# The place of the attention step in a unit of TensorE's queue: between the gate and the down products instead of behind the up products

## What is computed

```python
x = x + attn_ref(cond_ref(x, W1, b1, v, prompt), W_kv_down, W_k_up, W_v_up, W_q, W_q_rope, W_k_rope, W_o)
h = einsum('bsd,bdh->bsh', x, W[cats]) + b[cats][:, None, :]
...
def body(acc, ws):                       # over the 64 experts
    wg, wu, wdn, cw = ws
    hmid = silu(h @ wg) * (h @ wu)
    return (acc + cw[:, None] * (hmid @ wdn), None)
...
x = x + y + silu(h @ Ws_gate) * (h @ Ws_up) @ Ws_down
```

## Time and profile before

| what | us |
|---|---|
| runs | 753.29, 755.12, 757.13; median 755.12 |
| the profiled execution | 754.2 |
| its span, first to last instruction | 752.4 |
| PE busy in the span | 721.2 (96%) |
| DVE, ACT, POOL busy | 547.1, 453.3, 425.5 |
| mean granted clock of TensorE | 0.989 of full speed |

### The profile page before, as it was taken

The page is one execution under the profiler, slowest core; times in us unless marked ns, Lnnn a source line. Parts: engine busy times, 40 slices in busy tenths (PEclk is TensorE's granted clock), DMA queues, the critical chain, the costliest instruction groups (busy, mean ns, idle before and its releaser), DMA issues.

```text
span 752.4 us, 15834 instructions
## 1 busy us (share of the span) xinstructions
PE 721.2 (96%) x5644; PEld 556.2 (74%) x5644; DVE 547.1 (73%) x1150; ACT 453.3 (60%) x872; POOL 425.5 (57%) x349
## 2 busy tenths in 40 slices
PE   4788989999999999999999999999999999999997
PEld 3576767777787777777787777777777777877885
DVE  3867666886688856976778866888569766886664
ACT  2656875477555775567655775556755675555553
POOL 2456864555455655566455664566456555566665
PEclk8899999999999999999999999999999999999999
DMA  7494344434454364444545345443644344345451
GB/s 262 143 340 116 112 123 113 138 98 127 121 117 134 103 142 112 128 112 117 121 128 131 102 144 121 105 121 109 151 114 131 105 122 126 100 124 148 127 135 47
DMA packets 69055, 97.20 MB, mean 129 GB/s; under 512 B 8017, under 2 KB 26897, under 8 KB 68977
## 3 DMA queue, kind: packets, MB, share of 16 engines
q1 hardware_dynamic: 64512, 91.21, 44.8%
q10 hardware_dynamic: 4464, 4.98, 1.9%
HBM read 90.73 MB, written 4.98 MB: 127 GB/s over the span
## 4 chain that ended last, share of the span: by engine, by line
PE 75%; ACT 9%; DVE 8%; POOL 4%; issue 2%; DMA 1%; POOLq 0%; DVEq 0%; SPq 0%; ACTq 0%
PE Y L950 21%; PE U L950 20%; PE G L950 20%; PE A L950 12%; POOL hid_lo L613 2%; ACT s_t L378 2%; DVE act_w L921 2%; ACT hid_hi L517 2%; ACT L505 1%; DVE hid L933 1%; PE A L1011 1%; ACT L378 1%; ACT G L505 1%; DMA pooled_scratch<-hid 1%; DMA w<-in_weights 1%
## 5 line engine op out<-in xcount | busy, mean ns | idle before, releaser
L613 POOL TENSOR_TENSOR hid_lo<-hid,hid_hi 128x512 fp32r<-128x512 f32 (+1 forms) x264 | 342.2, 1296 | 277.5 <-ACT hid_hi L517 276.7
L921 DVE TENSOR_TENSOR act_w<-G,cwb 128x512 f32<-128x512 f32 x248 | 170.4, 687 | 99.8 <-ACT G L505 98.0
L505 ACT ACTIVATE G<-G 128x512 f32<-128x512 f32 x248 | 144.4, 582 | 149.3 <-PE G L950 147.5
L517 ACT CAST hid_hi<-hid 128x512 fp32r<-128x512 f32 (+1 forms) x264 | 162.3, 615 | 64.3 <-DVE hid L933 63.5
L933 DVE TENSOR_TENSOR hid<-act_w,U 128x512 f32<-128x512 f32 (+1 forms) x256 | 175.7, 686 | 23.4 <-PE Y L950 1.5
L950 PE MATMUL G<-c_hi,wg_hi 128*128 128x512 f32 x248 | 113.6, 458 | 0.0
L950 PE MATMUL Y<-hid_hi,wd_hi 128*128 128x512 f32 (+1 forms) x264 | 106.6, 404 | 5.3 <-POOL hid_lo L613 5.0
L950 PE MATMUL Y<-hid_hi,wd_lo 128*128 128x512 f32 (+1 forms) x264 | 103.5, 392 | 0.0
L950 PE MATMUL Y<-hid_lo,wd_hi 128*128 128x512 f32 (+1 forms) x264 | 103.5, 392 | 0.0
L950 PE MATMUL U<-c_hi,wu_hi 128*128 128x512 f32 x248 | 98.4, 397 | 0.0
L950 PE MATMUL G<-c_hi,wg_lo 128*128 128x512 f32 x248 | 97.7, 394 | 0.0
(11 more groups left out here) (183 smaller groups left out, 894.7 us busy)
## 6 DMA issues: line engine op xcount, KB each, us to landing
cwb<-cw_scratch SPq DMA_DIRECT2D x256, 256.0 KB, 3.7
k_blk<-in_cond_w SPq DMA_DIRECT2D x112, 64.0 KB, 2.3
wg_raw<-in_we_gate SPq DMA_DIRECT2D x8, 256.0 KB, 6.1
wu_raw<-in_we_up SPq DMA_DIRECT2D x8, 256.0 KB, 6.2
wd_raw<-in_we_down SPq DMA_DIRECT2D x8, 256.0 KB, 6.7
xf<-in_x_feat SPq DMA_DIRECT2D x8, 256.0 KB, 4.2
out_feat<-y ACTq DMA_DIRECT2D x8, 256.0 KB, 2.2
h_feat<-pooled_scratch SPq DMA_DIRECT2D x7, 256.0 KB, 2.7
```

The source lines that it names most:

```text
L505: nc.scalar.activation(gate_bank(p)[:, :], gate_bank(p)[:, :], ACT.Silu).then_inc(S["silu_done"], 1)
L517: nc.scalar.copy(hid_hi[0:n, p % NH, :], hid[0:n, p % NH, :]).then_inc(S["hi_ready"], 1)
L613: nc.gpsimd.tensor_sub(hid_lo[0:n, p % NH, :], hid[0:n, p % NH, :], hid_hi[0:n, p % NH, :].bitcast(F32)).then_inc(S["lo_ready"], 1)
L921: nc.vector.tensor_mul(act_w[:, p % NH, :], gate_bank(p)[:, :], cwb[:, p % NCW, :])\
```

## The change

In the PE part of a unit the two lines that issue the attention step move from the end of the unit to the place behind the gate product. Nothing else changes: the other engines keep their instructions and their order.

```diff
                 three(gate_bank(p)[:, :], wg_hi[:, p, :], wg_lo[:, p, :], c_hi[par][:, :], c_lo[par][:, :], True, True)\
                     .then_inc(S["gate_done"], 1)
+                for step, blk in steps_in(p, following, last):
+                    attention_step(step, blk)
                 if p >= NH:
                     down(b, p - NH)
                 elif prev:
                     down(b - 1, UNITS + p - NH)
...
                     three(up_bank(p)[:, :], wu_hi[:, p, :], wu_lo[:, p, :], c_hi[par][:, :], c_lo[par][:, :], True, True)\
                         .then_inc(S["up_done"], 1)
-                for step, blk in steps_in(p, following, last):
-                    attention_step(step, blk)
```

## The result

| | before | changed |
|---|---|---|
| median of 4 runs, us | 755.16 (753.29 to 757.13) | 793.37 (792.86 to 793.86) |
| ratio, 95% interval | | 1.0506 (1.0478 to 1.0533) |
| the profiled execution, us | 754.2 | 792.86 |
| its span, us | 752.4 | 791.0 |
| mean granted clock | 0.989 | 0.984 |

The account below looks back on a forecast made before the run. TensorE (PE), busy 721.2 of 752.4 us, was taken as the bound. Six later blocks at 5.46 us (32.8) plus 6.2 in the first gave 39.0 us on 754.2: 793 us, range 777 to 806.

Parts of the forecast that it names:

- step 17, att: Attention step in unit 12: PE waits 0.77 us for DVE's att, ready at E + 1.46; 0.11 added for the restart.
- step 19, x_next: Attention step: PE waits 0.89 us for DVE's result of the step before, ready at E + 1.58; 0.11 added.
- step 21, c: Attention step: PE waits 0.88 us for c, made by DVE one step earlier; 0.11 added for the restart.
- step 6, rope mask: Attention step in unit 1: PE waits 0.48 us for DVE's rope mask, ready at E + 1.17; 0.11 added.
- step 5, q_grp: Attention step in unit 0: PE waits 0.56 us for ACT's fourth q_grp, 0.67 with the restart.
- step 31, cw: PE waits 0.68 us for DVE's cw, kept late by routing; plus 0.11, less 0.10: 0.69.
- steps 13 and 14: Units 8 to 10: about 1.7 us wait for the first probability copy, partly given back at hid_lo; 0.64 us lost.
- E: Moment when a unit's up products have all been issued; PE was to reach the moved step at E + 0.69.
- the restart: PE's first product after a wait: 0.50 us long and not 0.39, so 0.11 added per wait, 0.44 for four.
- Only the DVE waits are real: Rival: the ACT and routing waits vanish, seven times 3.46 us stays: 778 us; chance 0.18.
- The clock falls: Rival: one clock fall of 1.5 us in each of seven blocks, 804 us, or 814 with a second; chance 0.12.
- Faster: Rival: earlier steps and later down products remove all hid_lo waits, 5.0 us: 749.2 us; chance 0.03.

Follow-up runs that it names:

- the fifth experiment: Changed kernel, with results PE waits for made ahead of hid on DVE and, for q_grp, ahead of the rounding on ACT: 771.42 us against 754.41, ratio 1.0219.
- eighth experiments: Kernel before the change, with only attention steps 16 to 21 moved behind the gate: 775.09 us against 756.27, ratio 1.0259.
- the third experiment: Kernel before the change, with only attention steps 5, 13, 14, 31 and 32, released by ACT or routing, moved behind the gate: 771.59 us, ratio 1.0197.
- the second experiment: Kernel before the change, with only attention steps 6, 17, 19 and 21, which wait for DVE, moved behind the gate: 765.81 us, ratio 1.0133.

## Why the prediction was right, point by point

The side, the mechanism and the time were right: 793 forecast, 793.37 measured. But the sum behind it was not right in every term. That the point was met to half a microsecond is luck: errors cancel. Per later block, in us:

| term | predicted | measured, by the gates |
|---|---|---|
| step 17, att | 0.88 | 0.78 |
| step 19, x_next | 1.00 | 0.79 |
| step 21, c | 0.99 | 0.86 |
| step 6, rope mask | 0.59 | 0.37 |
| step 5, q_grp | 0.67 | 0.68 |
| step 31, cw | 0.69 | 0.72 |
| steps 13 and 14 | 0.64 | 0.60 |
| the block | 5.46 | about 4.75 |

Small terms make up the rest of the last line: step 7 gives back 0.1 in unit 2, and steps 31 and 32 cost a little more in units 27 and 28.

**The waits themselves** came as written. Less the 0.16 us that the view hides, 0.77 (att), 0.89 (x_next), 0.88 (c), 0.48 (rope mask), 0.56 (q_grp) and 0.68 (cw) become 0.61, 0.73, 0.72, 0.32, 0.40 and 0.52; the brackets of the block shown above are 0.60, 0.70, 0.70, 0.30, 0.39 and 0.50. The fifth and eighth experiments tie them to DVE's and ACT's order and to the distance from E.

**The mis-sized terms of a later block** are the restart and the price of the waits at steps 6 and 19. For the restart the prediction says "so I add 0.11 to each". A 0.50 us product follows an attention step in either place: before, it was the gate behind the step, as in the earlier trace rows (360.27 and 364.11), now it is the down product. It was moved and not added. Of the four steps that wait for DVE only 17 and 21 take longer themselves behind their wait, by 0.06 and 0.10 from their start to the next group's: 0.16 us a block, and not 0.44. Steps 6 and 19 are rows of 32 small products. PE takes 0.32 us, and not 0.23, from the start of a 512-column product to the first of them in the kernel before too, where it waits for nothing:

```profile
377.27 0.39 PE L950 MATMUL U<-c_lo,wu_hi 128*128 128x512 f32 x1
...
377.59 1.08 PE L950 MATMUL A<-k_blk,x_next 128*32 128x128 f32 x32
```

So the wait there costs some 0.1 less than its length: 0.35 and not 0.48 at step 6, 0.77 and not 0.89 at step 19. The two together are most of the 0.7 by which a block was set too high.

**The first block** was set too high as well: 6.2 us, where 4.7 are measured without the fall of the clock (next paragraph). The 1.38 for "the products moved behind the wait" of step 13 left out that PE waited for hid_lo in front of the down products of units 7 and 8 in the kernel before, 0.25 us in the one and 0.69 in the other:

```profile
95.86 0.50 PE L950 MATMUL Y<-hid_hi,wd_hi 128*128 128x512 f32 x1 [0.69 <-POOL hid_lo L613]
```

These waits are gone in the changed kernel, so units 7 to 9 lose about 0.65 there and not 1.38.

**What made up for it.** The sum without these errors is 28.3 us in the later blocks and 4.7 in the first: 33 us, or 787. Two falls of the clock bring 4.0, and an opening that was 1.7 us longer in this execution the rest. The prediction had "so I take no fall", and a reading of 0.50 inside the blocks among its signs of a wrong sum; the sign came in two blocks. These are windows of the changed kernel at the fall in the first block (two), at that in a later one, and over steps 17 to 21 of this later block, where three waits follow one another without a fall:

```profile
100.00:101.00 1.00, 0.00 (x0) 0.00 (x0) 0.90 (x2) 1.00 (x3) 0.00 (x0) 0.56 0.00 0
...
104.00:107.00 3.00, 3.00 (x8) 2.29 (x8) 0.87 (x3) 0.00 (x0) 2.62 (x4) 0.51 0.70 154
...
380.00:382.50 2.50, 2.50 (x8) 1.92 (x7) 1.47 (x4) 1.10 (x2) 2.12 (x2) 0.50 0.63 176
...
393.00:406.00 13.00, 11.60 (x81) 8.67 (x79) 6.92 (x11) 5.79 (x11) 5.15 (x4) 1.00 0.39 102
```

The 0.5 in the first three is the level of 1.2 GHz; 0.56 is the mean of a stretch in which the clock falls. Both falls go with the wait of step 13. In the first block it begins while PE still waits, and PE then works at half speed: from the start of step 13 to that of step 14 PE takes 5.59 us (101.47 to 107.06), and 3.15 in a later block without a fall (286.80 to 289.95), so it costs 2.4 us. The later one costs 1.5: units 8 and 9 of its block are that much longer than in the others. The wait in the first block is

```profile
101.47 1.09 PE L1011 MATMUL A<-c,s_t 128*128 128x128 f32 x4 [4.08 <-ACT pt_sb L387]
```

It is longer than the 1.77 of the earlier trace rows by the down and up products that stood in front of it, which come behind it now, as the prediction says of the first block, and by the wait for hid_lo that stood in front of that down product.

**The rivals.** *Only the DVE waits are real* falls: the third experiment alone has 2.0 us a block from the others. *The clock falls* in every block falls as well: it fell in 2 of 7. *Faster* was wrong for the change as a whole, but the piece of it that the prediction names, the hid_lo waits, is there: they shrink from 5.0 to 1.3 us, and where steps 7 and 14 alone are moved and the copy comes first, the kernel gains 0.4 to 0.9%. *No effect* falls with the result.

**The expectation that missed by most**, 773 to 777 for the second experiment, failed by one step: the working took PE's arrival at E + 0.69 from the changed order, in which nothing but the gate lies between, and that held only if the step before is early as well.

## What to carry to other kernels

Before an instruction is moved forward in the queue of the engine that sets the pace, write down when its inputs are made and what that hangs on: if a result is made behind something that waits for the same engine's previous group, it needs a fixed time after that group, and the work in between is what hides it. Count the distance in issue times from that release and count every step that lies between. Where only some of the moved steps have inputs that are ready early, move those alone, and bring the late input forward on the engine that makes it.

## What the runs showed of the hardware

**The clock behind a wait isn't decided by the wait's length alone.** At the 4.1 us wait of the first block it fell in all three kernels that have it. Behind the wait of about 1.8 us that eight others have at the same place it fell in three and stayed at 1.00 in five, the kernel before among them; one of 2.5 us (step behind the down products) had no fall. At step 5 of the first block PE waits 1.4 to 2.5 us in every kernel; the clock fell there in ten of twelve, and stayed at 1.00 in two whose wait, 1.42 and 1.43 us, is no different from the 1.43 of three of the others. Of 18 waits of about 1.5 to 1.6 us at step 13 of later blocks one was followed by a fall. None of the waits of 0.6 to 0.7 us of units 12 to 16 was, though they come at every other unit. The Trainium skill, TensorE: Matmul & The Clock Gate, section "A second HAM failure mode: psum-queue depth-cycling", has frequent short idle stretches between groups of matmuls as a cause of such swings. Here the short waits that come often had no fall, and of the long ones only some; the runs leave open what decides among those.

**A small DVE instruction stood as long as POOL's.** In the fifth experiment cw, though made ahead of hid, came no earlier. One of its links, a TENSOR_SCALAR of 4 elements a partition, takes 0.76 us, and ends 0.03 us after a POOL instruction that was under way (414.26 and 414.23):

```profile
412.93 1.30 POOL L617 TENSOR_TENSOR hid_lo<-hid,hid_hi 128x512 fp32r<-128x512 f32 x1 [1.32 <-ACT hid_hi L517]
...
413.50 0.76 DVE L783 TENSOR_SCALAR small<-small 128x4 f32<-128x4 f32 x1
```

It is so in all seven blocks of that kernel. In the changed kernel the same instruction takes 0.27 us, but there it starts later in POOL's instruction, and it ends 0.02 us behind that one too (427.56 and 427.54). In the opening, where POOL has nothing under way, it takes 0.17:

```profile
426.24 1.29 POOL L613 TENSOR_TENSOR hid_lo<-hid,hid_hi 128x512 fp32r<-128x512 f32 x1 [1.32 <-ACT hid_hi L517]
...
427.29 0.27 DVE L779 TENSOR_SCALAR small<-small 128x4 f32<-128x4 f32 x1
...
62.34 0.17 DVE L779 TENSOR_SCALAR small<-small 128x4 f32<-128x4 f32 x1
```

In the 14 blocks of these two kernels it ends 0.02 to 0.04 us behind POOL's instruction, whenever it began. The Trainium skill, SBUF — State Buffer, section "SBUF: two separate sides", says that DVE and POOL share a pair of ports as an exclusive lock, which some DVE instructions need and which the other engine holds for its whole instruction. That would explain these ends; no run took POOL's instruction away from these places, so it is argued and not shown.

**The opening** takes between 68.1 and 73.5 us to the first gate from one kernel to the next, though none of them changes it. So differences of a few us need several runs, and a cause inside the blocks is better read from gate to gate.
